# One encoder layer in fp32 on one core: the merged query-key weights, the bias rows and two pairs' queries and scores computed from whole fp32 operands, and a new order of the front

## The reference, cut to what matters

```python
h = layernorm(x)
q = h @ Wq + bq;  k = ctx @ Wk + bk;  v = ctx @ Wv + bv
attn = softmax(q @ k.T * scale)
x = x + attn @ v
y = layernorm(x)
router, gate = softmax(y @ w_router), softmax(y @ w_gating / 0.1)
out_e = (silu(y @ w_gate[e]) * (y @ w_up[e])) @ w_down[e]       # all 8 experts
out = x + sum_e cw_e * out_e        # cw: normalised router * gate
```

## Time and profile before

| | us |
|---|---|
| median of 3 runs (973.61 to 974.1) | 973.72 |
| profiled execution | 973.45 |
| its span | 971.7 |
| TensorE busy | 965.2 (99%) |
| TensorE weight loads busy | 897.7 (92%) |
| GpSimd busy | 784.8 (81%) |
| VectorE busy | 744.4 (77%) |
| ScalarE busy | 484.8 (50%) |

### The profile page before, as it was taken

How to read it: one execution, slowest core, us unless ns; L and a number is a source line. 1 busy time by engine, 2 the same in 40 slices (tenths; PEclk the granted TensorE clock), 3 DMA queues, 4 the chain that set the end, 5 groups by cost and what they waited for, 6 DMA issues and landing times.

```text
span 971.7 us, 14884 instructions
## 1 busy us (share of the span) xinstructions
PE 965.2 (99%) x5188; PEld 897.7 (92%) x5188; DVE 744.4 (77%) x1278; ACT 484.8 (50%) x858; POOL 784.8 (81%) x619
## 2 busy tenths in 40 slices
PE   8999999999999999999999999999999999999998
PEld 7999899999999999999999999999999999999998
DVE  7987347777778777787877787777878777877886
ACT  6887554454444444444544444445445444444441
POOL 5699976776888888888988888888889888888852
PEclk9999999999999999999999999999999999999999
DMA  9342130411001111011100110011101200111202
GB/s 230 87 128 70 42 97 19 163 54 51 23 23 43 42 41 44 23 63 41 38 28 23 43 62 23 22 63 41 44 22 41 64 23 22 44 41 42 76 1 76
DMA packets 43426, 51.59 MB, mean 53 GB/s; under 512 B 2980, under 2 KB 39304, under 8 KB 43352
## 3 DMA queue, kind: packets, MB, share of 16 engines
q1 hardware_dynamic: 43344, 50.64, 17.1%
q10 hardware_dynamic: 8, 0.00, 0.0%
HBM read 45.07 MB, written 5.56 MB: 52 GB/s over the span
## 4 chain that ended last, share of the span: by engine, by line
PE 98%; DMA 1%; ACT 0%; SPq 0%; issue 0%; DVE 0%; DVEq 0%
PE ps L318 95%; PE ps L1711 1%; DMA shared<-in_ctx 1%; PE ps L1739 1%; PE ps L1700 0%; PE ps L1756 0%; PE ps L1782 0%; PE ps L1945 0%; ACT arena L808 0%; PE ps L1812 0%; PE ps L1807 0%; ACT early L744 0%; DVE arena L322 0%; SPq L362 0%; ACT arena L763 0%
## 5 line engine op out<-in xcount | busy, mean ns | idle before, releaser
L318 PE MATMUL ps<-arena 128*128 128x448 f32 (+5 forms) x2112 | 395.4, 338 | 1.3 <-DVE arena L322 1.3
L318 PEld LDWEIGHTS ps<-arena 128*128 128x128 f32 (+2 forms) x2112 | 350.6, 186 | 23.0 <-DVE arena L1193 1.1
L566 POOL TENSOR_TENSOR arena<-shared,arena 128x448 fp32r<-128x448 f32 x196 | 252.9, 1304 | 130.1 <-ACT arena L930 127.1
L318 PE MATMUL ps<-xc_hi,w_hi 128*128 128x448 f32 x904 | 331.8, 367 | 0.0
L318 PE MATMUL ps<-xc_hi,w_lo 128*128 128x448 f32 x904 | 330.2, 365 | 0.0
L318 PE MATMUL ps<-xc_lo,w_hi 128*128 128x448 f32 x904 | 330.1, 365 | 0.0
L318 PEld LDWEIGHTS ps<-xc_hi,w_hi 128*128 128x128 f32 x904 | 169.9, 188 | 14.0 <-DVE cw_rows L1397 0.4
L318 PEld LDWEIGHTS ps<-xc_hi,w_lo 128*128 128x128 f32 x904 | 169.8, 188 | 13.6
L318 PEld LDWEIGHTS ps<-xc_lo,w_hi 128*128 128x128 f32 x904 | 169.9, 188 | 12.9
L923 ACT ACTIVATE shared<-shared 128x448 f32<-128x448 f32 x180 | 101.5, 580 | 146.4 <-DVE shared L1306 74.5
L679 POOL TENSOR_TENSOR xsacc<-xsacc,xf 128x448 f32<-128x448 f32 x104 | 119.2, 1158 | 0.0
(11 more groups left out here) (164 smaller groups left out, 1147.7 us busy)
## 6 DMA issues: line engine op xcount, KB each, us to landing
early<-in_L_ffn_w_down SPq DMA_DIRECT2D x16, 512.0 KB, 3.9
xf<-cw_dram SPq DMA_DIRECT2D x16, 448.0 KB, 4.7
shared<-in_ctx SPq DMA_DIRECT2D x16, 336.0 KB
w_raw<-in_L_ffn_w_gate SPq DMA_DIRECT2D x17, 256.0 KB, 2.9
w_raw<-in_L_ffn_w_up SPq DMA_DIRECT2D x17, 256.0 KB, 3.2
early<-in_L_ffn_w_gate SPq DMA_DIRECT2D x15, 256.0 KB, 2.8
early<-in_L_ffn_w_up SPq DMA_DIRECT2D x15, 256.0 KB, 3.2
x_dram<-xsacc SPq DMA_DIRECT2D x8, 224.0 KB, 3.1
```

The source lines that it names most:

```text
L318: ins = nc.tensor.matmul(dst, w, m, start=first and i == 0, stop=last and i == len(passes) - 1, skip_group_check=onto)
L566: nc.gpsimd.tensor_tensor(h[:, 1, j, at:at + TC], tile, h[:, 0, j, at:at + TC].bitcast(fp32), ALU.subtract).then_inc(hid_lo_done, 1)
```

## The change

- `FULL = 2`: pairs 0 and 1 keep x transposed, ctx transposed and the queries as whole fp32 tiles (`xt_full`, `ct_full`, `q_full`). `queries` and `scores` of these pairs are whole fp32 matmuls, one for each of the two 128-row halves, in place of three fp32r passes. `xt_low`, `ct_low` and `q_low` are gone for these pairs. `split_or_kept` makes the waits: for pairs 0 and 1 on the copy, later on the `lo` tile.
- Wq^T and Wk^T are kept whole (`wqt`, `wkt`); `weights_low` is gone. M is made from them by whole fp32 matmuls, kept whole (`m_full`) and used whole by pairs 0 and 1. Its `hi` copy is one more ScalarE instruction, its `lo` moves from VectorE to GpSimd (`m_low`), and both are first needed by pair 2.
- The three bias products use whole operands too; the bias splits and `vb_sum` are gone.
- x is loaded in eight DMAs by pair (four before), and its statistics and inverse roots are made by pair: eight `stats1` and eight `root1` (five before).
- `wqt`, `wkt`, `m_full` and `xt_full` lie in `w_raw0`, so `load_set(0)` now waits for `m_low`, for the queries of pair 1 and for `both_biases`.
- The orders of all five lists up to the loop are new. The number of `keep_busy` is again ten: four (three before) stand ahead of the biases, one follows `key_bias_row`, one (two before) follows `queries(0)`, none stands ahead of `scores(0, 0)` or `scores(1, 0)`, and two (one before) stand ahead of `transpose_ctx(3, 0)`. The loop is unchanged.

```diff
+    FULL = 2
+        ct_full = xf_f[:, 0:at0].rearrange("p (b k n) -> p b k n", b=2, k=DK)
+        q_full = xf_f[:, at0 + TQ:at0 + TQ + DK * TP].rearrange("p (k t) -> p k t", k=DK)
+        wqt, wkt, m_full = [w_raw0_f[:, i * DK * D:(i + 1) * DK * D].rearrange("p (k n) -> p k n", k=DK) for i in range(3)]
+        xt_full = w_raw0_f[:, 3 * DK * D:3 * DK * D + DK * TP].rearrange("p (k t) -> p k t", k=DK)
...
+        def split_or_kept(engine, high, low, i, full):
+            if i < full:
+                engine.wait_ge(high, i + 1)
+            else:
+                engine.wait_ge(low, i + 1 - full)
...
             def load_set(n):
+                if n == 0:
+                    sp.wait_ge(m_lo_done, 1)
+                    sp.wait_ge(q_ready, FULL)
+                    sp.wait_ge(c0_ready, 1)
...
+            def m_low():        # GpSimd
+                pool.wait_ge(m_hi_done, 1)
+                nc.gpsimd.tensor_tensor(m_lo, m_full, m_hi.bitcast(fp32), ALU.subtract).then_inc(m_lo_done, 1)
...
+                nc.scalar.mul(m_full, ps_m, -SCALE).then_inc(m_kept, 1)
...
-                nc.scalar.mul(m_hi, ps_m, -SCALE).then_inc(m_hi_done, 1)
+                nc.scalar.copy(m_hi, m_full).then_inc(m_hi_done, 1)
...
             def merged_weights():
-                pe.wait_ge(wt_lo_done, 2)
+                pe.wait_ge(wt_kept, 2)
...
-                    ins = accumulate(ps_m[:, it, :], [t for et in range(DK) for t in
-                                                      three(wqt_hi[:, et, cols], wqt_lo[:, et, cols], wkt_hi[:, et, :], wkt_lo[:, et, :])])
+                    ins = accumulate(ps_m[:, it, :], [(wqt[:, et, cols], wkt[:, et, :]) for et in range(DK)])
...
             def queries(p):
-                pe.wait_ge(xt_lo_done, p + 1)
+                split_or_kept(pe, xt_hi_done, xt_lo_done, p, FULL)
...
+                    if p < FULL:
+                        passes = [(m_full[:, k, cols], xt_full[:, k, :]) for k in range(DK)]
...
             def scores(p, b):
-                pe.wait_ge(q_lo_done, p + 1)
-                pe.wait_ge(ct_lo_done, 2 * p + b + 1)
+                split_or_kept(pe, q_hi_done, q_lo_done, p, FULL)
+                split_or_kept(pe, ct_hi_done, ct_lo_done, 2 * p + b, 2 * FULL)
...
+                if p < FULL:
+                    passes = [(q_full[:, k, rows], ct_full[:, b, k, 0:TK]) for k in range(DK)]
```

More of the change, by code:

```diff
@@ L615, in _ @@
             cn_low(5, 0)
-            add_bv(6)
             cn_low(5, 1)
@@ L639, in _ @@
             sum_of_set(3, 3)
+            root2(5)
+            norm2(5)
+            plain_low(0, 0)
+            add_bv(7)
             root2(6)
-            plain_low(0, 0)
+            plain_low(0, 1)
             norm2(6)
-            plain_low(0, 1)
+            low_part(1, "first")
             root2(7)
@@ L945, in _ @@
-            xt_high(1)
-            cn_high(1, 1)
-            high_set(0)
             ct_high(1, 0)
             exponentials(0, 0)
-            q_high(1)
-            pt_high(0, 0)
+            xt_high(1)
             ct_high(1, 1)
             exponentials(0, 1)
+            pt_high(0, 0)
+            q_high(1)
             pt_high(0, 1)
+            norm1(2)
+            cn_high(1, 1)
+            xt_high(2)
+            wv_high()
             ct_high(2, 0)
-            norm1(2)
             exponentials(1, 0)
-            wv_high()
@@ L973, in _ @@
             exponentials(2, 0)
+            cn_high(3, 0)
+            ct_high(3, 1)
+            pt_high(2, 0)
             exponentials(2, 1)
+            q_high(3)
+            cn_high(3, 1)
+            pt_high(2, 1)
             normalise(1)
[L976 to L981, removed]
             norm1(4)
             ct_high(4, 0)
-            cn_high(3, 1)
+            at_high(1)
@@ L985, in _ @@
             xt_high(4)
+            high_set(1)
             exponentials(3, 0)
-            at_high(1)
+            normalise(2)
+            ct_high(4, 1)
             exponentials(3, 1)
+            q_high(4)
+            pt_high(3, 0)
+            norm1(5)
+            pt_high(3, 1)
             cn_high(4, 0)
[L990 to L995, removed]
+            xt_high(5)
+            cn_high(4, 1)
@@ L996, in _ @@
+            router_high()
             ct_high(5, 0)
             exponentials(4, 0)
-            xt_high(5)
+            cn_high(5, 0)
+            keep_norm2(0)
             at_high(2)
-            cn_high(4, 1)
+            ct_high(5, 1)
             exponentials(4, 1)
-            ct_high(5, 1)
-            keep_norm2(0)
             pt_high(4, 0)
+            q_high(5)
+            norm1(6)
+            pt_high(4, 1)
             normalise(3)
-            q_high(5)
-            cn_high(5, 0)
@@ L1008, in _ @@
-            pt_high(4, 1)
-            norm1(6)
+            cn_high(5, 1)
+            ct_high(6, 0)
             at_high(3)
-            cn_high(5, 1)
+            keep_norm2(1)
             xt_high(6)
-            ct_high(6, 0)
             exponentials(5, 0)
+            high_part(0, "first")
+            cn_high(6, 0)
             exponentials(5, 1)
+            normalise(4)
+            pt_high(5, 0)
             ct_high(6, 1)
-            pt_high(5, 0)
-            keep_norm2(1)
-            normalise(4)
+            pt_high(5, 1)
@@ L1020, in _ @@
             q_high(6)
-            cn_high(6, 0)
-            pt_high(5, 1)
             at_high(4)
+            keep_norm2(2)
             norm1(7)
             cn_high(6, 1)
+            cn_high(7, 0)
+            ct_high(7, 0)
+            normalise(5)
+            cn_high(7, 1)
             xt_high(7)
-            keep_norm2(2)
-            ct_high(7, 0)
             exponentials(6, 0)
-            high_part(0, "first")
+            keep_norm2(3)
+            at_high(5)
             exponentials(6, 1)
+            pt_high(6, 0)
@@ L1032, in _ @@
+            high_part(0, "second")
+            pt_high(6, 1)
             q_high(7)
[L1033 to L1037, removed]
+            high_part(0, "s2")
             ct_high(7, 1)
[L1039 to L1042, removed]
+            high_part(0, "s13")
             normalise(6)
-            high_part(0, "s13")
             exponentials(7, 0)
@@ L1134, in stats1 @@
             def stats1(i):
-                first, end, part = ((0, 2, 0), (2, 4, 1), (4, 8, 2), (8, 12, 3), (12, B, 3))[i]
-                ve.wait_ge(x_parts[part], DMA)
+                first, end = 2 * i, 2 * i + 2
+                ve.wait_ge(x_parts[i], DMA)
                 ve.wait_ge(eps_set, 1)
@@ L2031, in _ @@
             mix_ctx(2)
+            transpose_ctx(4, 1)
+            queries(4)
             transpose_probs(3, 0)
-            queries(4)
-            transpose_ctx(4, 1)
+            transpose_mix(2)
+            values(1)
             transpose_probs(3, 1)
-            values(1)
-            scores(4, 0)
-            transpose_mix(2)
             transpose_ctx(5, 0)
             transpose_norm(5)
+            scores(4, 0)
+            mix_ctx(3)
+            transpose_norm2(0)
             scores(4, 1)
-            mix_ctx(3)
@@ L2068, in _ @@
+            transpose_norm(7)
+            values(4)
+            scores(6, 1)
+            transpose_mix(5)
+            transpose_norm2(3)
+            transpose_ctx(7, 1)
+            transpose_probs(6, 0)
             queries(7)
-            transpose_probs(6, 0)
-            values(4)
             transpose_probs(6, 1)
-            transpose_mix(5)
-            transpose_ctx(7, 1)
+            values(5)
+            mix_ctx(6)
             scores(7, 0)
-            transpose_norm2(3)
-            mix_ctx(6)
```

524 lines of the change are left out of this document (254 added, 270 removed).

## The result

| | before | after |
|---|---|---|
| median of 11 runs, us | 973.72 | 971.18 |
| profiled execution, us | 973.45 | 970.92 |
| its span, us | 971.7 | 969.0 |
| start of `transpose_ctx(3, 0)`, us | 33.59 | 30.90 |

The ratio is 0.9975, with a 95% interval from 0.9965 to 0.9985. The kernel became 2.5 us faster; 1.2 us were forecast.

What follows compares the result with a forecast made beforehand. Bound: TensorE's work plus its waits at both ends. `transpose_ctx(3, 0)` 1.2 us earlier, +0.9 of work included and other moves booked 0: 973.45 minus 1.2 is 972.25; median 0.27 above, so 972.5; range 970.4 to 975.4.

Steps and rivals of the forecast that it cites:

- rival A: Front up to `transpose_ctx(3, 0)`: all front stalls gone, start about 31.0, 2.6 us earlier, 971.1 us; chance 0.25.
- a first shift outside 0 to 2.6: Sign that the prediction is wrong: `transpose_ctx(3, 0)` starts earlier by an amount outside 0 to 2.6 us.
- TensorE's work: Front matmuls with whole operands: `scores` +0.97, `queries` +0.16, `merged_weights` +0.23, `key_bias_row` -0.48; sum about +0.9 us.
- Rival D: New wide whole matmuls: fp32 weight loads show, +3.8 us on the forecast, 976.3 us; chance 0.07.
- The clock: Program start: first 6 to 7 us at half rate, so the fourth `keep_busy` costs 0.8 us and shifts both weight transposes.
- step 1: Weights: second transposes end at 7.2, `key_bias_row` at 8.1, `query_bias` at 9.3, `merged_weights` at 11.7 (before: 10.7).
- step 5: From `transpose_probs(1, 0)` to `transpose_ctx(3, 0)`, which starts at 32.4, 1.2 us earlier than before.
- steps 3 and 4: ScalarE sets the chain, `cn_high` 0.8 and `q_high` 0.79: `scores(0, 0)` starts at 16.0, `mix_ctx(0)` ends at 28.1.
- TensorE stands still for 1.3 us after 15, and ScalarE ends every wait: Front after 15 us: 0.3 before `scores(0, 0)`, 0.3 before each of two others, 0.1 here and there.
- B: Front: the work comes, the chain does not shorten, `merged_weights` ends 1 us later; 974.6 us; chance 0.13.
- C: Between 35 and 130 us: GpSimd becomes the wait, about 3.6 us late, 976.1 us; chance 0.10.
- The 5.6 us that I added to GpSimd: Between 30 and 160 us: `m_low`, `root1` and `low_set(0)` add 5.6, where GpSimd idles 19.85 of 130; booked 0.

Runs made afterwards that it cites:

- after_plus10: Changed kernel with ten more `keep_busy` behind `transpose_norm(3)`, ahead of `mix_ctx(1)`: 974.2 to 975.34 us, ratio 1.0011.
- before_again: The kernel before, unchanged, run once more for a second trace: 973.66 us in the only run.
- after_again: The changed kernel, nothing altered, run once more: 970.55 to 971.5 us, ratio 0.997.
- before_4kb: The kernel before with a fourth `keep_busy` ahead of the biases: 973.32 to 974.21 us.
- before_whole2: Whole operands in the kernel before's list orders, with `m_low`, set 0 and set 1 steps placed anew to remove two waits: ratio 1.0023.
- after_full3: Changed kernel with `FULL = 3`, so pair 2 is whole too: 972.78 to 975.53 us.
- after_full0: Changed kernel with `FULL = 0`: new orders, but x, ctx and queries of pairs 0 and 1 split again: 976.41 to 977.29 us.
- before_whole: Whole operands in the kernel before's list orders, with `m_low` ahead of `wv_low` and `load_set(0)` behind `load_ctx(3, 0)`: 985.56 to 986.64 us.

## Why the prediction was right, and where its size was off

The direction, the place and the way to count held. The point at which to compare, `transpose_ctx(3, 0)`, carries the whole difference (2.69 of 2.7), and after_plus10 shows that little behind it absorbs or adds. 971.18 lies in the stated range, but not because the forecast came true. What came was rival A: PE's waits shrank to the start alone, the point at 30.90 where A said 31.0, the time 971.18 where A said 971.1. A had a chance of 0.25 beside 0.45 for the forecast, and a time below 971.8 had 0.30 beside 0.55 for no visible change. By one of its own signs, a first shift outside 0 to 2.6, the prediction fails: 2.69, and 2.79 between before_again and after_again. With the execution of after_plus10 the shift is 2.0, so this sign is decided by the chance in the moment of the full rate.

- **TensorE's work.** +0.24 per `scores` was +0.27 (1.31, 1.31, 1.27), +0.08 per `queries` was +0.12 (1.59, 1.53), `merged_weights` 1.74 was 1.73, `key_bias_row` 0.96 was 0.87. The twelve split passes of the last, booked at 1.44, took 1.21 where they ran at the full rate, in before_4kb:

```profile
7.20 1.37 PE L318 MATMUL ps<-xc_hi,arena 128*112 128x128 f32 x12 [0.36 <-DVE xc_hi L322]
8.41 0.82 PE L1711 MATMUL ps<-ident,shared 125*128 125x125 f32 x6
```

So the saving there is 0.34 and not 0.48, and the sum is +1.2 where +0.9 was forecast. This error went against the gain. Rival D falls: the loads do not show. Its price was counted for 16 wide matmuls, and with the four of `merged_weights` there are 20, so it should have been 1 us higher. The estimate from the Trainium skill ("TensorE: Matmul & The Clock Gate", Back-to-back issue gap), 1.27 for a whole `scores`, agrees with the trace within 0.04.
- **The clock** is the first mis-sized term, in step 1. I carried the half rate to the end of the second weight transposes, at 7.2, and the fourth `keep_busy` at 0.8, where 0.74 is right (the first three last from 1.15 to 3.66, 2.51 and not 2.41, in the kernel before; the first four of the change from 1.15 to 4.40). In the profiled execution the transposes ended at 6.55: 0.65 us of the 1.5 by which step 5 (32.4 against 30.90) was late. It is partly chance, as the rate rises anywhere between 4.5 and 7.1.
- **ScalarE's steps** are the second, in steps 3 and 4. I added lengths of rows where start distances count. ACT's timeline of the changed kernel:

```profile
13.44 0.83 ACT L843 CAST arena<-shared 125x768 fp32r<-125x768 f32 x1
14.17 0.79 ACT L798 ACTIVATE xf<-ps,qbias 128x224 f32<-128x224 f32 x2
14.84 0.84 ACT L843 CAST arena<-shared 125x768 fp32r<-125x768 f32 x1
15.57 1.10 ACT L779 ACTIVATE early<-xsacc,bias,rstd 112x256 f32<-112x256 f32 x2
```

From start to start a `cn_high` occupies ScalarE for 0.73, not the 0.8 that I booked, and `q_high` for 0.67, not 0.79. The trace is 0.8 us ahead of my walk at `queries(0)`, 1.0 at `scores(0, 0)` (15.01 against 16.0) and 1.5 at the end. I put most of what comes behind `queries(0)` down to some 0.1 on each ScalarE step; no run shows this term alone. I had read TensorE by start distances, and not the engine that I named as the bound. `both_biases`, booked at 0.5 and in fact 0.33 (12.04 to 12.37), is a small third.
- **TensorE stands still for 1.3 us after 15, and ScalarE ends every wait** was wrong: behind the start the table names no wait of PE at all. What is left of it is a wait of the weight loads for `norm1(2)`, which PE does not feel, as `scores(1, 0)` in front of it takes 1.27 like the others:

```profile
22.85 0.50 PEld L1710 LDWEIGHTS ps<-ident,early 112*128 112x128 f32 x4 [0.28 <-ACT early L779]
```

- **Rivals B and C.** before_whole2 comes near B's result, since the lead of 1.0 us at `queries(0)` is spent at `transpose_ctx(3, 0)`, but not by B's mechanism, a late `merged_weights`. C does not happen in the change, where no PE wait names GpSimd; in before_whole2 it costs 1.68. The 5.6 us that I added to GpSimd between 30 and 160 were 1.0 (110.15 to 111.15): `m_low` and most `root1` fall before 30. So the idle share that I had given as cover was not put to the test in the change, and in before_whole2, with 110.99 us busy, it did not keep a wait away.

## What to carry to other kernels

Where one engine is full behind the front, compare two versions by the start of the first step after which it is full, and price every change at that step. Whole fp32 matmuls in place of three split passes cost TensorE 0.1 to 0.3 us here for each `scores`, `queries` or `merged_weights`. They paid in a latency chain, and only together with lists reordered so that the shorter chain is used: each half alone, as I placed it, lost 0.1 to 0.2%. A semaphore condition on one DMA holds up the loads behind it in the queue, as after_full3 shows (x of pair 6 issued at 30.22 in place of 24.53). When you walk a chain, add start distances on every engine.

## What the runs showed of the hardware

- The moment at which TensorE reaches the full rate differs between executions by 2.6 us (4.5 to 7.1 us), while the granted clock in the windows reads 1.00. At the start of the program only the durations of identical instructions show it. It may be one source of the spread of the changed kernel (970.59 to 971.57); that was not measured execution by execution.
- Without `keep_busy` the half rate lasted from 3.65 to about 12 us, again with 1.00 in the windows. Later in a program the granted clock does show a fall. An idle stretch of 2.14 us was followed by six passes of `scores` at half rate (after_full0, 0.59 from 26 to 29 us), one of 2.01 us by half rate from 34.7 to 38.5 (before_whole, 0.55), and one of 1.68 us by none (before_whole2, 1.00 from 61.2 to 64).
- A whole fp32 matmul appears as two MATMUL and two LDWEIGHTS rows. At 375 columns it takes 0.64 to 0.65, at 224 columns 0.38 to 0.40, at 256 columns 0.43, and its weight loads stay hidden. At 128 columns it takes 0.22, about as long as its two loads (0.93 for eight in `key_bias_row`), and at one column 0.16 to 0.20.
